# A fused transformer kernel on one core: transposes of gathered rows in another order, and three steps of VectorE moved ahead of a weight split

## The chip, the cores and the metric

The kernel runs on one core of one Trainium2 chip. The metric is the device time of one execution in microseconds (us). A core has a matmul engine (TensorE, PE in the profile; its weight loads are PEld), VectorE (DVE), ScalarE (ACT), GpSimd (POOL), SyncE (SP), which issues most DMAs, and 16 DMA engines. The engines run their own instruction streams and meet at semaphores.

## What is computed

`x` has 512 tokens of 1024 values. Three layers are added to it: attention to a context, a gated layer with ternary weights, and the one that matters here, a mixture of eight experts with a shared expert, in float32:

```python
x = x + xattn(layernorm(x), ctx)
x = x + bit_ffn(layernorm(x))
x = x + ffn(layernorm(x))

def ffn(x):                        # T = 512, D = 1024, E = 8, F = 512, K = 2
    h = rmsnorm(x)
    probs = softmax(h @ router_w)
    topv, topi = top_k(probs, 2);  topv = topv / sum(topv)
    g, u = h @ w_gate[e], h @ w_up[e]            # for each expert e
    eo = (silu(g) * u) @ w_down[e]
    moe = sum_e w_dense[:, e] * eo               # only the two chosen experts count
    sh = (silu(h @ sw_gate) * (h @ sw_up)) @ sw_down
    return moe + sh
```

## The kernel before

Each float32 matrix product is made of parts of lower precision: an operand is split into a high part (`WH`, the halves `EX[:, k, 0]` and `HTH`, copied by ACT) and a residue (`WL`, `EX[:, k, 1]`, `HTL`, made by DVE as the operand minus its high part), and PE multiplies high by high, high by low and low by high.

The expert layer works in tiles. There are four shared tiles of 128 tokens (the last of them at the end of the kernel, after the routed ones) and, with these inputs, eight routed tiles, one for each expert, of up to R = 160 gathered rows. The rows of a routed tile lie in device memory; SP loads 128 of them into `XG` and the other 32 (`TAIL_R`) into a quarter of `XY` (`XTAIL`). The order of the work is written out by hand, engine by engine, with semaphores in between.

A routed tile on PE (`routed_tile`, line 2005): the gate products into PSUM banks 0, 1, 3, 4, the up products beside them (lines 2013 to 2020), then the transposes of the *next* tile's rows (`routed_rows`, line 1940), then the down products (lines 2028 to 2044). The transposes write in three groups, `TK` = chunks 0 to 2, 3 to 5, and 6 and 7, into banks `TB` = 0, 1, 3, which the gate and up results must have left: DVE's `routed_product` (line 1027) reads them in three steps and raises `hsum` to 3 (banks 0 and 1 free), 4 (bank 3) and 5. `routed_rows` transposes 8 chunks of `XG` (line 1944, 128 rows each), then 8 chunks of the 32 rows in `XY` (line 1947), and raises `et_pe` after the first group's `XY` part and at the end. ACT copies the groups to `EX` (`routed_hi`, line 1572; the first waits for the first `et_pe`, the second for the other), DVE makes their residues (`routed_lo`, line 1014).

A routed tile on DVE (`tile`, line 1212): sums, result of the tile before, products, `routed_hidden_lo`, `routed_lo`; after it the six halves of the next expert's weight residues (`split`, line 1000). Each half is 128x2048 and raises `free_c[j]` (j = 0, 1 gate, 2, 3 up, 4, 5 down). SP's load of the following expert's half j waits for `free_c[j]`, and so do PE's products: gate for `free_c0` and `free_c1`, up for `free_c2` and `free_c3`, down for the last two.

The entry to the routed tiles is written out apart. The third shared tile is tile NS - 1 = 2. Its hidden values go to `HTKH` and `HTKL` and are kept for the end of the kernel. On PE its gate and up products are followed by the transposes of the first routed tile's rows (into banks `TB_FIRST` = 4, 5, 3) and of its own hidden values `HE` (line 1995). On DVE, lines 1202 to 1209:

```python
            split(1, 2)
            split(1, 0, (0,))
            e.wait_ge(s("rows"), 1)
            split(1, 0, (1,))
            hidden_product(NS - 1)
            routed_lo(NS, TB_FIRST)
            hidden_lo(NS - 1, HTKH, HTKL)
            split(1, 1)
```

`hidden_product` makes `HE` (line 1054), `hidden_lo` the residue `HTKL` (line 1062), `hidden` is one and then the other. ACT's `hidden` (line 1599) does the Silu, the high parts of the gate weights, the copies of `routed_hi` and then those to `HTKH` (line 1607), then splits the up weights.

Of the kernel before, what the change touches and what calls it, by code (L numbers as in the profile page):

```python
# [21 lines left out]
P = 128  # L22
# [12 lines left out]
NS = 3  # L35
R = 160
# [42 lines left out]
def program(nc, x, ctxT, wv, wqk, wo, wbit, n_gate, n_down, n_rms, wrt, wmoe, out, rows_dram):  # L79
    es = ExitStack()  # L80
    with es:
# [186 lines left out]
        def s(name):  # L268
            if name not in S:
                S[name] = sem(name)  # L270
            return S[name]
# [415 lines left out]
        def _(e):  # L687
# [515 lines left out]
            split(1, 0, (0,))  # L1203
            e.wait_ge(s("rows"), 1)
            split(1, 0, (1,))
            hidden_product(NS - 1)
            routed_lo(NS, TB_FIRST)
            hidden_lo(NS - 1, HTKH, HTKL)
            split(1, 1)
# [56 lines left out]
        def _(e):  # L1266
# [370 lines left out]
            e.wait_ge(s("ys_d"), NS)  # L1637
            e.wait_ge(s("ht_lo"), 2 * NS)
            e.wait_ge(s("cnt"), 1)
# [18 lines left out]
        def _(e):  # L1658
# [280 lines left out]

            def routed_rows(t, at=TB):  # L1940
                waits(e, ("e_in", t * 32 + 32))
                for n, ks in enumerate(TK):
                    for i, k in enumerate(ks):
                        e.transpose(bank[at[n]][:, i * R:i * R + P], XG[:, k * P:k * P + P], IDF[:, :])
                for n, ks in enumerate(TK):
                    for i, k in enumerate(ks):
                        m = e.transpose(bank[at[n]][:, i * R + P:i * R + R], XY[XTAIL, k * P:k * P + P], IDF[XTAIL, XTAIL])
                    if n != 1:
                        m.then_inc(s("et_pe"), 1)
# [11 lines left out]
            def tile(t, n, gi):  # L1961
# [18 lines left out]
                if n < NS - 1:  # L1980
                    rows_t(0, H3[:, n + 1, :])
                elif more:
                    e.wait_ge(s("ys_d"), NS)
                    routed_rows(NS, TB_FIRST)
                else:
                    waits(e, ("ys_a", t + 1), ("ys_d", t + 1), (free_c[4], gi + 1), (free_c[5], gi + 1))
                    kept_result(HT1H, HT1L, 2)
# [17 lines left out]
            def routed_tile(t, gi):  # L2005

                waits(e, ("et_lo", t * 2 + 2))
                for m in range(2):
                    waits(e, (free_c[2 * m], gi + 1), (free_c[2 * m + 1], gi + 1))
                    for f in range(KE):  # L2010
# [10 lines left out]
                        if m:  # L2021
                            mm.then_inc(s("up_pe"), 1)
                        elif f % 2:
                            mm.then_inc(s("gate_pe"), 1)
                waits(e, ("hsum", t * 5 + 4))
                routed_rows(t + 1)
                waits(e, ("ys_a", t + 1), ("ys_d", t + 1), (free_c[4], gi + 1), (free_c[5], gi + 1))
# [123 lines left out]
```

## Time and profile before

| what | us |
|---|---|
| median of 3 executions | 652.65 |
| lowest, highest | 651.95, 652.75 |
| the profiled execution: its time | 652.65 |
| its span | 650.9 |
| PE busy | 619.1 |
| DVE busy | 512.7 |
| ACT busy | 423.5 |
| POOL busy | 147.4 |

PEclk is the granted clock of TensorE as a share of 2.4 GHz (0.50 is 1.2 GHz). The time is that of the whole execution; the span runs from the first to the last recorded instruction. A busy engine is one with an instruction under way, and the ends of matmuls are modelled, so rows of PE may overlap: the start of one to the start of the next is the step to read. In a timeline row, equal instructions in a row are merged: start, time from the first start to the last end, engine, line, operation, output and inputs, active rows and columns, count. A bracket behind it tells the idle time of that engine ahead of it and what ended it; without a bracket there was none that counts.

### The profile page before, as it was taken

Reading aid. Unit: us, or ns where it says so; the run is one execution under the profiler, and the core shown is the slowest. Engines: PE = TensorE matmul, PEld = TensorE weight load, DVE = VectorE, ACT = ScalarE, POOL = GpSimd, SP = SyncE. Lnnn points to the kernel's source line nnn. Section 1 sums busy time; section 2 is a strip of 40 time slices with the busy share of each in tenths; the row PEclk is TensorE's granted clock in tenths of the full one; section 3 lists DMA queues with packets and bytes.
Section 4 is the critical chain, followed back from the end, with each engine's and each line's share of the span. In section 5 each row is a group of like instructions: output and inputs, shape, how many; then the busy total and the mean of one; then the engine's idle time right before and its main releaser. Section 6 shows DMA issues by size and latency. Waiting matters only on the chain.

```text
span 650.9 us, 10573 instructions
## 1 busy us (share of the span) xinstructions
PE 619.1 (95%) x3676; PEld 481.8 (74%) x3677; DVE 512.7 (79%) x861; ACT 423.5 (65%) x559; POOL 147.4 (23%) x146
## 2 busy tenths in 40 slices
PE   5889999998999999969999998999999999999996
PEld 4678888886887444434557888898988989889775
DVE  5787777889587779989899467678796887968686
ACT  3888888789656969885475355547375573755630
POOL 3363445426000333518900310000000000000051
PEclk9999999999999999989999998999999999999999
DMA  8967776765246999736999548595775957759247
GB/s 332 408 260 298 294 298 234 299 260 191 98 152 265 416 366 349 287 129 244 416 371 358 211 184 307 223 393 193 297 297 207 391 201 300 285 221 380 88 163 264
DMA packets 31068, 177.87 MB, mean 273 GB/s; under 512 B 4064, under 2 KB 4064, under 8 KB 14784
## 3 DMA queue, kind: packets, MB, share of 16 engines
q1 hardware_dynamic: 25536, 158.64, 63.1%
q0 software_dynamic: 5504, 18.88, 7.7%
q8 instruction: 15, 0.25, 0.2%
q14 instruction: 13, 0.11, 0.1%
HBM read 154.30 MB, written 23.20 MB: 273 GB/s over the span
## 4 chain that ended last, share of the span: by engine, by line
PE 58%; DVE 16%; ACT 13%; issue 5%; DMA 5%; POOL 1%; SPq 1%; DVEq 0%; POOLq 0%; ACTq 0%
PE BK L2017 14%; PE BK L305 9%; PE BK L2020 5%; ACT PR L1350 5%; PE BK L311 4%; PE BK L1757 4%; PE BK L312 3%; PE BK L317 3%; PE BK L1858 3%; PE BK L2040 2%; DVE WL L1004 2%; DMA RA<-wbit 2%; PE BK L2039 2%; DMA RX<-wqk 2%; DVE BH L886 1%
## 5 line engine op out<-in xcount | busy, mean ns | idle before, releaser
L2017 PE MATMUL BK<-EX,WH 128*128 128x320 f32 x512 | 133.3, 344 | 1.8 <-DVE EX L1017 1.8
L2020 PE MATMUL BK<-EX,WL 128*128 128x160 f32 x448 | 106.3, 237 | 0.0
L1004 DVE TENSOR_TENSOR WL<-RA,WH 128x2048 fp32r<-128x2048 f32 x40 | 89.3, 2286 | 9.4 <-ACT WH L1535 9.2
L2017 PEld LDWEIGHTS BK<-EX,WH 128*128 128x128 f32 x512 | 93.0, 190 | 2.7 <-issue 2.0
L2020 PEld LDWEIGHTS BK<-EX,WL 128*128 128x128 f32 x448 | 86.3, 193 | 0.3
L1535 ACT ACTIVATE WH<-RA 128x2048 fp32r<-128x2048 f32 x40 | 73.7, 1920 | 2.2 <-PE BK L1858 2.2
L681 POOL DMA_INDIRECT GA<-rows,SLOT x4 | 4.9, 1228 | 248.4 <-DVE WL L1004 247.4
L649 POOL TENSOR_TENSOR HB<-HB,ND (+2 forms) x28 | 31.1, 1128 | 104.7 <-DVE BH L886 104.0
L1420 ACT ACTIVATE RA<-RA,RT 128x2048 int16<-128x2048 f32 x22 | 44.2, 2019 | 9.4 <-DMA RA<-wbit 6.4
L1004 DVE TENSOR_TENSOR WL<-RC,WH 128x2048 fp32r<-128x2048 f32 x20 | 44.9, 2284 | 0.7 <-ACT WH L1535 0.7
L1626 ACT ACTIVATE HX<-SR 128x320 fp32r<-128x320 f32 x16 | 7.5, 471 | 54.0 <-DVE SR L1035 54.0
L1812 PE MATMUL BK<-TG,XQ 128*128 128x512 bf16 x192 | 42.4, 379 | 0.1
L1535 ACT ACTIVATE WH<-RC 128x2048 fp32r<-128x2048 f32 x20 | 37.3, 1907 | 7.5 <-PE BK L2040 6.8
L1858 PE MATMUL BK<-TD,HQT 128*128 128x512 bf16 x176 | 39.8, 387 | 0.0
L1032 DVE TENSOR_TENSOR UT<-BK,SR 128x160 f32<-128x160 f32 (+1 forms) x24 | 9.1, 380 | 35.6 <-PE BK L2017 35.6
L1350 ACT ACTIVATE PR<-BK,RT 128x512 f32<-128x512 f32 (+1 forms) x64 | 32.7, 536 | 6.6 <-DVE RT L753 6.6
L1323 ACT ACTIVATE RA<-RA 128x2048 f32<-128x2048 f32 x19 | 36.2, 1910 | 0.0
L1812 PEld LDWEIGHTS BK<-TG,XQ 128*128 128x128 bf16 x192 | 18.6, 98 | 22.5 <-ACT XQ L1413 0.6
L1812 PE MATMUL BK<-TX,XQ 128*128 128x512 bf16 x160 | 35.2, 379 | 0.0
L607 POOL TENSOR_TENSOR WQH<-RA,ONEF 128x768 fp32r<-128x768 f32 (+1 forms) x14 | 22.0, 1574 | 51.1 <-DMA RA<-wqk 43.3
L1858 PEld LDWEIGHTS BK<-TD,HQT 128*128 128x128 bf16 x176 | 17.4, 100 | 20.7 <-issue 1.4
L1812 PEld LDWEIGHTS BK<-TX,XQ 128*128 128x128 bf16 x160 | 15.7, 98 | 18.9
(305 smaller groups left out, 1582.2 us busy)
## 6 DMA issues: line engine op xcount, KB each, us to landing
RA<-wbit SPq DMA_DIRECT2D x54, 1024.0 KB, 6.4
RA<-wmoe SPq DMA_DIRECT2D x40, 1024.0 KB, 6.8
RC<-wmoe SPq DMA_DIRECT2D x20, 1024.0 KB, 7.5
rows<-ZERO POOLq DMA_DIRECT2D x40, 256.0 KB, 12.8
XG<-rows SPq DMA_DIRECT2D x10, 512.0 KB, 3.7
rows<-YS SPq DMA_DIRECT2D x9, 512.0 KB, 6.0
RA<-wqk SPq DMA_DIRECT2D x7, 640.0 KB, 7.8
RA<-wo SPq DMA_DIRECT2D x4, 1024.0 KB, 7.4
```

What stands on the lines that cost most here:

```text
L305: m = e.matmul(dst, st, mv, start=first and i == 0 and j == 0, stop=last and i == n - 1 and j == 2)
L311: e.matmul(dst, sh, mh, start=first and i == 0, stop=False)
L649: e.tensor_tensor(HB[:, t, cs], HB[:, t, cs], ND[:, cs], ALU.mult).then_inc(s("hnd"), 1)
L1004: e.tensor_tensor(WL[m][:, q * RAW:q * RAW + RAW], RC[j][:, :], WH[m][:, q * RAW:q * RAW + RAW].bitcast(f32), ALU.subtract)\
L1323: e.activation(RA[j][:, :], RA[j][:, :], ACT.Abs, accum_out=ACCW[:, column]).then_inc(free_a[j], 1)
L1350: ins = e.activation(PR[h][:, off:off + P * (i + 1)], STR[h][:, off:off + P * (i + 1)], ACT.Exp, bias=NM[:, h, i:i + 1], accum_out=RS[:, h ...
L1420: e.activation(RB16[j], RB[j][:, :], ACT.Copy, scale=SW[:, 0:1]).then_inc(s("rnd"), 1)
L1535: e.activation(WH[m][:, q * RAW:q * RAW + RAW], RC[2 * m + q][:, :], ACT.Copy)\
L1812: m = e.matmul(bank[out], XQ[:, k, t * P:t * P + P], weights[:, k, :], start=k == 0, stop=k == KD - 1)
L1858: m = e.matmul(bank[2 * (t % 2) + q], HQT[t % 2][:, k, :], (TD1[:, k, :] if k < 16 else TD2[:, k - 16, :])[:, q * 512:q * 512 + 512], star ...
L2017: mm = e.matmul(bank[GBK[f]][:, 0:2 * R], WH[m][:, at], EX[:, k, :, :].rearrange("p a b -> p (a b)"), start=k == 0, stop=k == KD - 1)
L2020: e.matmul(bank[GBK[f]][:, 0:R], WL[m][:, at], EX[:, k, 0, :], start=False, stop=False)
```

## The change

Three places are edited.

1. On PE, `routed_rows` takes the groups it is to do. Within a group each 128-row transpose of `XG` is now followed by the 32-row transpose of `XY` for the same chunk. In a routed tile the first two groups wait for `hsum` 3 and the third for `hsum` 4; before, all waited for `hsum` 4. At the entry all three groups run in one go.
2. On DVE, at the entry, `hidden_product`, `hidden_lo` and `routed_lo`, in this order, stand ahead of the second half of the gate weights' residue; before, that half came first, and `hidden_lo` last.
3. On ACT, a wait for `ht_lo` ahead of the routed tiles is gone.

```diff
--- before.py
+++ after.py
@@ -1202,10 +1202,9 @@
             split(1, 2)
             split(1, 0, (0,))
             e.wait_ge(s("rows"), 1)
+            hidden(NS - 1, HTKH, HTKL)
+            routed_lo(NS, TB_FIRST)
             split(1, 0, (1,))
-            hidden_product(NS - 1)
-            routed_lo(NS, TB_FIRST)
-            hidden_lo(NS - 1, HTKH, HTKL)
             split(1, 1)
             e.sem_inc(s("hsum"), 5 * NS)
 
@@ -1635,7 +1634,6 @@
             e.sem_inc(s("ys_a"), NS)
             split(1, NS, (1,))
             e.wait_ge(s("ys_d"), NS)
-            e.wait_ge(s("ht_lo"), 2 * NS)
             e.wait_ge(s("cnt"), 1)
             with e.Fori(1, NE) as gi:
                 n, t0 = group_of(e, gi)
@@ -1937,14 +1935,14 @@
                     m = e.transpose(bank[4 + q][:, k * P:k * P + P], rows[:, cs], IDF[:, :])
                 m.then_inc(s("et_pe"), 1)
 
-            def routed_rows(t, at=TB):
-                waits(e, ("e_in", t * 32 + 32))
-                for n, ks in enumerate(TK):
-                    for i, k in enumerate(ks):
-                        e.transpose(bank[at[n]][:, i * R:i * R + P], XG[:, k * P:k * P + P], IDF[:, :])
-                for n, ks in enumerate(TK):
-                    for i, k in enumerate(ks):
-                        m = e.transpose(bank[at[n]][:, i * R + P:i * R + R], XY[XTAIL, k * P:k * P + P], IDF[XTAIL, XTAIL])
+            def routed_rows(t, ns, at=TB):
+                for n in ns:
+                    if n == 0:
+                        waits(e, ("e_in", t * 32 + 32))
+                    for i, k in enumerate(TK[n]):
+                        cs = slice(k * P, k * P + P)
+                        e.transpose(bank[at[n]][:, i * R:i * R + P], XG[:, cs], IDF[:, :])
+                        m = e.transpose(bank[at[n]][:, i * R + P:i * R + R], XY[XTAIL, cs], IDF[XTAIL, XTAIL])
                     if n != 1:
                         m.then_inc(s("et_pe"), 1)
             def routing(step):
@@ -1981,7 +1979,7 @@
                     rows_t(0, H3[:, n + 1, :])
                 elif more:
                     e.wait_ge(s("ys_d"), NS)
-                    routed_rows(NS, TB_FIRST)
+                    routed_rows(NS, (0, 1, 2), TB_FIRST)
                 else:
                     waits(e, ("ys_a", t + 1), ("ys_d", t + 1), (free_c[4], gi + 1), (free_c[5], gi + 1))
                     kept_result(HT1H, HT1L, 2)
@@ -2022,8 +2020,10 @@
                             mm.then_inc(s("up_pe"), 1)
                         elif f % 2:
                             mm.then_inc(s("gate_pe"), 1)
+                waits(e, ("hsum", t * 5 + 3))
+                routed_rows(t + 1, (0, 1))
                 waits(e, ("hsum", t * 5 + 4))
-                routed_rows(t + 1)
+                routed_rows(t + 1, (2,))
                 waits(e, ("ys_a", t + 1), ("ys_d", t + 1), (free_c[4], gi + 1), (free_c[5], gi + 1))
                 for h in range(2):
                     waits(e, ("ht_hi", t * 2 + h + 1))
```

PE, in the loop over the routed tiles: from the last up product (L2017, L2020) over the transposes (XG: L1944, XY: L1947) to the first down product (L311). Before:

```order
843 L2017 MATMUL BK<-EX,WH_140 128x320
844 L358 REGISTER_ALU
845 L358 ISA [waits hsum]
846 L1944 MATMUL BK<-IDF,XG 128x128 [waits e_in]
847 L1944 MATMUL BK<-IDF,XG 128x128 x7
848 L1947 MATMUL BK<-IDF,XY 128x32 x8
849 L358 REGISTER_ALU [waits free_c4,free_c5,ys_d,ys_a]
850 L311 MATMUL BK<-WH_141,HX 128x512 [waits ht_hi]
```

After, the last pair of the second group, the third group and the first down product (XY is now line 1945). Ahead of these rows stand `hsum` 3, `e_in` and five pairs like the first one here:

```order
869 L1944 MATMUL BK<-IDF,XG 128x128
870 L1945 MATMUL BK<-IDF,XY 128x32
871 L358 REGISTER_ALU
872 L1944 MATMUL BK<-IDF,XG 128x128 [waits hsum]
873 L1945 MATMUL BK<-IDF,XY 128x32
874 L1944 MATMUL BK<-IDF,XG 128x128
875 L1945 MATMUL BK<-IDF,XY 128x32
876 L358 REGISTER_ALU [waits free_c4,free_c5,ys_d,ys_a]
877 L311 MATMUL BK<-WH_141,HX 128x512 [waits ht_hi]
```

Eight 128-row and eight 32-row transposes in two runs have become sixteen that alternate, with a wait before the seventh pair.

DVE, at the entry, between the weight residues of the gate (WL_146) and of the up weights (WL_150). Before:

```order
460 L1004 TENSOR_TENSOR WL_146<-RA_95,WH_145 128x2048 [waits m_hi]
461 L1004 TENSOR_TENSOR WL_146<-RA_96,WH_145 128x2048 [waits m_hi,rows]
462 L1054 TENSOR_TENSOR HE<-BK,SI 128x256 [waits up_pe,gate_a]
463 L1054 TENSOR_TENSOR HE<-BK,SI 128x256
464 L1017 TENSOR_TENSOR EX<-BK,EX 128x3x160 [waits et_hi] x2
465 L1017 TENSOR_TENSOR EX<-BK,EX 128x2x160 [waits et_hi]
466 L1062 TENSOR_TENSOR HTKL<-BK,HTKH 128x256 [waits ht_hi] x2
467 L1004 TENSOR_TENSOR WL_150<-RA_97,WH_140 128x2048 [waits m_hi]
468 L1004 TENSOR_TENSOR WL_150<-RA_98,WH_140 128x2048 [waits m_hi]
```

After:

```order
460 L1004 TENSOR_TENSOR WL_146<-RA_95,WH_145 128x2048 [waits m_hi]
461 L1054 TENSOR_TENSOR HE<-BK,SI 128x256 [waits up_pe,gate_a,rows]
462 L1054 TENSOR_TENSOR HE<-BK,SI 128x256
463 L1062 TENSOR_TENSOR HTKL<-BK,HTKH 128x256 [waits ht_hi] x2
464 L1017 TENSOR_TENSOR EX<-BK,EX 128x3x160 [waits et_hi] x2
465 L1017 TENSOR_TENSOR EX<-BK,EX 128x2x160 [waits et_hi]
466 L1004 TENSOR_TENSOR WL_146<-RA_96,WH_145 128x2048 [waits m_hi]
467 L1004 TENSOR_TENSOR WL_150<-RA_97,WH_140 128x2048 [waits m_hi]
468 L1004 TENSOR_TENSOR WL_150<-RA_98,WH_140 128x2048 [waits m_hi]
```

The second WL_146 row went from ahead of HE to behind EX, and HTKL from behind EX to ahead of it.

## Rows read from the trace of the kernel before

**Rows 1.** The page, part 1: busy time, share of the span, instructions.

```profile
PE 619.1 (95%) x3676; PEld 481.8 (74%) x3677; DVE 512.7 (79%) x861; ACT 423.5 (65%) x559; POOL 147.4 (23%) x146
```

**Rows 2.** Waits from 386 us: us in total, times, longest us.

```profile
PE BK L2017 <- DVE EX L1017: 1.8, 1, 1.8
...
PEld BK L1947 <- issue: 1.5, 9, 0.2
```

**Rows 3.** Lines from 400 us: busy us, mean ns | idle before us.

```profile
L2017 PE MATMUL BK<-EX,WH 128*128 128x320 f32 x501 | 129.0, 342 | 0.0
```

**Rows 4.** Lines 1944 and 1947: durations, first and last start.

```profile
L1944 PE MATMUL BK<-IDF,XG x72: 270/272/273, 390.7 to 605.7; 128*128 128x128 f32 x72
...
L1947 PE MATMUL BK<-IDF,XY x72: 220/222/243, 391.7 to 606.3; 32*128 32x32 f32 x72
```

**Rows 5.** Timeline, PE, first routed tile: start, us, engine, line, what.

```profile
413.56 1.04 PE L1944 MATMUL BK<-IDF,XG 128*128 128x128 f32 x8
...
414.53 0.68 PE L1947 MATMUL BK<-IDF,XY 32*128 32x32 f32 x8
...
415.14 0.50 PE L311 MATMUL BK<-WH,HX 128*128 128x512 f32 x1
```

**Rows 6.** Timeline, PE, around the 8-row transposes of the logits.

```profile
354.39 0.39 PE L311 MATMUL BK<-WH,EX 128*128 128x512 f32 x1
354.61 0.39 PE L312 MATMUL BK<-WL,EX 128*128 128x512 f32 x1
354.93 0.41 PE L1919 MATMUL BK<-IDF,HE 8*128 8x8 f32 x4
355.27 0.50 PE L311 MATMUL BK<-WH,EX 128*128 128x512 f32 x1
```

**Rows 7.** Timeline, ACT, first routed tile.

```profile
414.71 0.47 ACT L1626 ACTIVATE HX<-SR 128x320 fp32r<-128x320 f32 x1 [3.15 <-DVE SR L1035]
415.09 1.34 ACT L1576 ACTIVATE EX<-BK 128x480 fp32r<-128x480 f32 x3
```

**Rows 8.** Timeline, DVE and PE, the next expert's weight splits and its first product.

```profile
418.27 6.70 DVE L1004 TENSOR_TENSOR WL<-RA,WH 128x2048 fp32r<-128x2048 f32 x3 [0.89 <-ACT WH L1535]
...
424.43 0.31 PE L2017 MATMUL BK<-EX,WH 128*128 128x320 f32 x1
```

**Rows 9.** Timeline, PE, entry to the routed tiles.

```profile
390.72 1.03 PE L1944 MATMUL BK<-IDF,XG 128*128 128x128 f32 x8
...
392.82 0.77 PE L1995 MATMUL BK<-IDF,HE 128*128 128x128 f32 x4 [0.46 <-DVE HE L1054]
395.43 0.38 PE L2017 MATMUL BK<-EX,WH 128*128 128x320 f32 x1 [1.84 <-DVE EX L1017]
```

**Rows 10.** Timeline, DVE, entry to the routed tiles.

```profile
387.94 4.50 DVE L1004 TENSOR_TENSOR WL<-RA,WH 128x2048 fp32r<-128x2048 f32 x2 [1.57 <-ACT WH L1535]
392.35 0.75 DVE L1054 TENSOR_TENSOR HE<-BK,SI 128x256 f32<-128x256 f32 x2
393.01 1.61 DVE L1017 TENSOR_TENSOR EX<-BK,EX 128x480 fp32r<-128x480 f32 x3
394.54 0.75 DVE L1062 TENSOR_TENSOR HTKL<-BK,HTKH 128x256 fp32r<-128x256 f32 x2
```

**Rows 11.** Timeline, ACT, entry to the routed tiles.

```profile
392.08 1.36 ACT L1576 ACTIVATE EX<-BK 128x480 fp32r<-128x480 f32 x3 [2.38 <-PE BK L1947]
393.32 0.69 ACT L1607 ACTIVATE HTKH<-BK 128x256 fp32r<-128x256 f32 x2
...
401.40 0.44 ACT L1616 ACTIVATE SR<-BK 128x320 f32<-128x320 f32 x1 [2.23 <-PE BK L2017]
```

**Rows 12.** Stretch: length, PE busy (count), PEclk, DMA share, GB/s; then timeline, PE.

```profile
396.05:399.46 3.41, 3.41 (x17) 0.50 0.95 352
288.53:293.65 5.12, 4.95 (x28) 0.50 0.47 195
...
288.53 3.04 PE L1852 MATMUL BK<-IDB,HQ 128*128 128x128 bf16 x22 [5.22 <-DVE HQ L990]
```

## The prediction

> **What bounds the kernel now.** I read the page first, then the list of waits, then the timeline at the two places that the diff touches. TensorE is busy for 95% of the span [rows 1], so only what stands between its matmuls, or what it issues itself, can move the time much. In the waits from 386 us on there is one real wait of the matmul queue near the change: 1.8 us ahead of the first product of the first routed tile. The other entry, 1.5 us in nine pieces ahead of the loads of the 32-row transposes, is put down to "issue", that is, to nothing that another engine did [rows 2]. In the lines from 400 us on, the routed products have no idle time before them [rows 3]. So the eight routed tiles, one for each expert, run on TensorE without a wait. For them, semaphores set earlier buy nothing; a nanosecond more in TensorE's own stream is paid eight times.
>
> **Part 1: the order of the transposes in a routed tile.** Before, PE issues 8 transposes of XG (128 rows) and then 8 of XY (32 rows). The XG ones start at 413.56 and span 1.04 us; one lasts 0.272 us [rows 4], so seven steps take 0.77 us, 0.11 us each, and the last starts at 414.33. The XY ones start at 414.53 and span 0.68 us with 0.222 us each: 0.066 us a step, the last at 414.99. The next product starts at 415.14 [rows 5]. From first transpose to next product: 1.58 us. Now look at the two seams. From the last XG to the first XY there are 0.20 us where a step is 0.11, from the last XY to the next product 0.15 us where a step is 0.066. Each change of the number of active rows costs about 0.09 us. That this belongs to the row count, and not to this place, shows elsewhere. The 8-row transposes of HE start 0.32 us after the last 128x512 product, where such products follow each other at 0.23 us: again 0.09. On the way back, (0.41 - 0.20)/3 = 0.07 us a step puts the last one at 355.14, and the next product comes at 355.27: 0.13 where a step is 0.07, so 0.06 [rows 6].
>
> The change makes the order XG, XY, XG, XY and so on: 15 seams inside the block and one behind it, where there were 1 and 1. That is 14 more. At 0.09 us: +1.26 us for a tile, and the block takes 2.84 us instead of 1.58. It lies on the path, because TensorE is what everything else waits for. Eight tiles: **+10.1 us**. Bounds: nothing, if the seams hide when they alternate (rival A); the 0.06 of the 8-row case for the seven additional ways back, 7 x 0.03 x 8 = 1.7 us less. Above: the second XY after a seam may itself be slow, but in the new order there is no second one; I let the upper bound be 1 us more. I take 0.09 because both seams of these very instructions show it.
>
> The Trainium skill, page "TensorEngine Tiling (Array Packing)", section "Tiling Modes", Key Properties, says that changing the tiling mode, "not just tile", drains TensorE. By that rule every seam of a 128-row and a 32-row instruction costs, as the rows have it; the page gives no price, and the 0.09 us is the trace's.
>
> **Part 2: the earlier wait in a routed tile.** The first six transpose pairs wait for `hsum` 3 instead of 4, the last two pairs for 4. The old wait never held PE: the transposes at 413.56 have no idle time before them [rows 5]. The gain is 0. The added wait stands in the middle of PE's stream, with the down products queued behind it. Its cost lies between 0 and the 0.17 us of an issue gap [rows 2], 0 to 1.4 us over eight tiles; the similar wait in the middle of the up products (line 2012, with L2017 right behind it) leaves L2017 no idle time at all from 400 us on [rows 3], so I take **+0.2 us** in all.
>
> Who profits from the first `et_pe` coming earlier? ACT can copy the first group only after its own HX copy, which waits for DVE until 414.71 and lasts to 415.18; the EX copies follow at once at 415.09 [rows 7]. So an increment before 415.09 is worth nothing. The second `et_pe` comes when all pairs are done, 1.26 us later than now; ACT's second and third copy, and DVE's, end about 1.0 us later. What they hold up next is the split of the next expert's gate weights: DVE runs three halves in 6.70 us from 418.27, so the second ends near 422.8, and PE needs it at 424.43 [rows 8]: 1.6 us of slack. DVE moves by 1.0 us, PE by 1.26: the slack stays. Cost 0. It would be lost only if DVE came 1.9 us later.
>
> **Part 3: the entry to the routed tiles.** Before: PE ends the shared tile, does the 16 routed transposes from 390.72, waits 0.46 us for HE, transposes HE at 392.82 and stands idle for 1.84 us until 395.43 [rows 9]. DVE runs two weight halves 387.94 to 392.44, then HE 0.75 us, the EX residues 1.61 us, the HTK residues 0.75 us [rows 10]. ACT copies EX 392.08 to 393.44 and HTKH 393.32 to 394.01 [rows 11].
>
> Now the second weight half (gate weights, `free_c1`) stands behind all of that, and PE's first routed product waits for `free_c0`, `free_c1` and `et_lo`. Working forward:
> - DVE ends the first half near 390.2. HE needs the shared tile's up product, which ends when the transposes begin to run, near 390.9, so HE is done at 391.7, 1.4 us earlier.
> - PE: pairs at 0.35 us from 390.72. The third pair's XY starts at 391.63 and ends at 391.85 (first `et_pe`); the eighth's starts at 390.72 + 7 x 0.35 + 0.20 = 393.4 and ends at 393.6 (second `et_pe`). The HE transposes follow at 393.54 and are through at 393.9 and 394.15.
> - ACT: first EX copy 391.9 to 392.4; the other two from 393.65 to 394.5; HTKH to 394.8 and 395.15.
> - DVE waits for HTKH, since its residues are now first in the queue: HTKL 394.9 to 395.6, EX residues to 397.15, the weight half (4.50 / 2 = 2.25 us) to 399.4.
> - PE starts at 399.5 instead of 395.43: **+4.05 us**.
>
> Queued behind on DVE are the two halves of the up weights, which then end near 404; PE needs them after all gate products, of which the first half alone took from 395.43 to 401.40 [rows 9, 11], so not before 405.5: nothing. On SP the load of the next expert's second weight half waits for `free_c1` and moves by 7 us, with four loads behind it; they are issued by about 404, and DVE's splits use them only from 418.27 on [rows 8]. Nothing. The wait that ACT loses (`ht_lo`) held nothing: ACT's next work followed its own split without idle time.
>
> **The clock.** After the 1.84 us gap the granted clock was 0.50 from 396.05 to 399.46: 3.4 us, half of it lost, 1.7 us. After the 5.22 us gap ahead of 288.53 it was 0.50 until 293.65: 5.1 us of work, 2.5 us lost [rows 12]. The new gap is 394.15 to 399.5, 5.3 us, nearest to the second. The difference is +0.8 us; the step down need not fall at the same point of the work, so -0.9 to +1.0; I take **+0.5 us**.
>
> **Sum.** The profiled execution took 652.65 us, its span is 650.9, and 652.65 is also the median, so no correction is needed. 652.65 + 10.1 + 0.2 + 4.05 + 0.5 = **667.5 us**. The end of the kernel (the copies of the last tile's result, its store, the gathers) waits for PE's last routed tile and shifts with it.
>
> **Rivals.**
> A. *The seams hide.* Alternating loads could be brought in under the running transpose, and a pair would cost no more than 0.11 + 0.066. For it: at both places the trace has one seam each way, never a row of them. Against: the loss shows at every seam. Then the tiles cost nothing and the entry is shorter (transposes done at 392.4, HTKH at 393.9, the EX residues at 395.9, the weight half at 398.1): +2.8 + 0.5, 656.0 us. The Trainium skill, "TensorE: Matmul & The Clock Gate", "Step-by-step: what each phase is for", says that weight loads are pulled ahead of running matmuls when row groups do not conflict or the load goes to the background buffer; taken alone, that gives this case. 7%.
> B. *The clock falls in the routed tiles too.* The block would have 2.84 us of short instructions with gaps. The clock did fall after thin work at the entry. Against: there PE had idle time of 0.46 and 1.84 us, here gaps of 0.09. One fall of 3.4 us a tile costs 1.7 us, eight cost 13.7: 681 us; a few of them, 670 to 675. 9%.
> C. *Faster.* If alternating lets each XY transpose run under the load of the next XG one, a pair costs little more than the 0.11 of its XG part, say 0.13: a block takes about 1.1 us, -0.5 us a tile, -4.0 in all, against +2.8 at the entry with no change of the clock: 651.4 us. It wins from 0.35 us a tile on, that is, a pair under 0.155 us. Against it: the seams cost, they don't save. 2%, and 1% for a time within the bound of no change.
> D. *The entry does not move as worked out*, for instance because PE's own scalar loads ahead of the loop, and not DVE, held it until 395.43. That would not help: DVE's half ends at 399.4 either way. It is inside the range.
>
> **How the numbers follow.** The forecast, 81%: 667.5 us. Within it: seams -1.7 to +1, the added wait -0.2 to +1.2, the clock -1.4 to +0.5, the entry +-0.5. Not all fall on one side, so 663.8 to 671; A and C lie below, most of B above. What a measurement of this kernel can tell from no change is about 0.2%, 1.3 us. Slower 0.97 (forecast, A, B), same 0.01, faster 0.02.
>
> **What would show it.** In the trace after: between the first XG transpose of a routed tile and the first down product 2.8 us instead of 1.58, starts of XG and XY alternating at 0.20 and 0.15 us; the distance of two routed tiles 28.6 instead of 27.3 us (now: the last XG transpose of all starts at 605.7 [rows 4], its block 0.77 us earlier, seven tiles behind 413.56); the first routed product about 4 us later, released by the DVE weight split and not by EX; DVE idle ahead of HTKL for some 3 us; the granted clock 1 in all routed tiles but the first. Wrong: pairs at 0.18 us, or DVE's weight splits being what PE waits for at later tiles.

## The result

| | us |
|---|---|
| before, median of 4 | 652.7 (651.95 to 653.28) |
| after, median of 4 | 684.38 (683.93 to 686.18) |
| ratio | 1.0491, 95% interval 1.0469 to 1.0514 |
| after, the profiled execution: its time, its span | 685.42, 683.6 |

The change makes the kernel 31.7 us slower. The forecast was 667.5 us and the range ended at 671: the direction and the two places were right, the size was half of what came. The cause that I had as rival B, at 9%, came true in every tile, and the price of a seam (the place in TensorE's stream where 128-row and 32-row instructions meet) was too low.

The page of the profile after, PE's busy time and the granted clock in 40 slices. Against [rows 1] PE is busy 30 us longer, as 95% of a longer span. The 7 in the second half of the clock's row is the entry to the routed tiles. The falls in the tiles can't be seen in this row: one of 3.4 us takes a tenth from a slice of 17.1 us, and 9 stands for 90% or more. They show only in shorter stretches, further down.

```profile
PE 649.1 (95%) x3663; PEld 498.8 (73%) x3677; DVE 513.6 (75%) x861; ACT 424.6 (62%) x559; POOL 148.3 (22%) x146
...
PEclk9999999999999999899999979999999999999999
```

The waits from 386 us on (engine, line, waited for: us in total, times, longest). PE's one wait at the entry has grown from the 1.8 us of [rows 2] to 5.3, and its releaser is now the weight split. ACT now waits for PE's transposes in every tile, 15.4 us in all with the entry. In the tiles that costs nothing, since no routed product behind the entry waits for it, but it shows how late the second `et_pe` is.

```profile
ACT EX L1575 <- PE BK L1945: 15.4, 10, 2.4
...
PE BK L2015 <- DVE WL L1004: 5.3, 1, 5.3
```

PE in the first routed tile: start, us, line. Where [rows 5] had eight and eight, each instruction now stands alone.

```profile
419.63 0.27 PE L1944 MATMUL BK<-IDF,XG 128*128 128x128 f32 x1
419.83 0.24 PE L1945 MATMUL BK<-IDF,XY 32*128 32x32 f32 x1
420.01 0.33 PE L1944 MATMUL BK<-IDF,XG 128*128 128x128 f32 x1
420.27 0.24 PE L1945 MATMUL BK<-IDF,XY 32*128 32x32 f32 x1
...
422.87 0.24 PE L1945 MATMUL BK<-IDF,XY 32*128 32x32 f32 x1
423.05 0.50 PE L311 MATMUL BK<-WH,HX 128*128 128x512 f32 x1
```

From 419.63 to 423.05 are 3.42 us where there were 1.58. The first XG to XY is 0.20 us, as I had reckoned; XY to XG is 0.18 instead of 0.15, and every later XG to XY is 0.26 instead of 0.20. A pair costs 0.435 us, not 0.35. The XG transposes themselves are recorded longer, 0.328 us in the median against 0.272 [rows 4]: each but the first of a block now comes right behind a change of the row count.

```profile
L1944 PE MATMUL BK<-IDF,XG x72: 270/328/331, 390.7 to 637.7; 128*128 128x128 f32 x72
```

The last of these starts at 637.7; its block began 3.04 us (seven pairs) earlier, at 634.7, so seven tiles take (634.7 - 419.6) / 7 = 30.7 us each, where they took 27.3. Of the 3.4 us more, 1.84 are the block. The other 1.55 are the clock. Stretches of PE (length, busy and count, granted clock, DMA share, GB/s):

```profile
400.05:406.60 6.55, 6.55 (x27) 0.50 0.90 331
406.60:423.60 17.00, 17.00 (x120) 1.00 0.61 241
423.60:427.00 3.40, 3.40 (x10) 0.51 0.57 192
427.10:454.40 27.30, 27.30 (x178) 1.00 0.68 254
454.40:457.80 3.40, 3.40 (x10) 0.50 0.63 193
```

After the entry the clock is 0.50 for 6.55 us of work, against 3.4 us in [rows 12]. Then it falls behind the first block, from 423.6 to 427.0, is 1 again, falls from 454.4 to 457.8, and so on: eight falls behind eight blocks, the last at 638.7. Each begins 4.0 us after the first transpose of its block, behind the first full products, and holds 3.4 us of work at half the clock. In the trace before there was none between 399.5 and the end of the tiles.

The entry, against [rows 10], [rows 11] and [rows 9]: DVE, ACT, PE.

```profile
391.00 0.76 DVE L1054 TENSOR_TENSOR HE<-BK,SI 128x256 f32<-128x256 f32 x2 [0.79 <-PE BK L317]
395.43 0.76 DVE L1062 TENSOR_TENSOR HTKL<-BK,HTKH 128x256 fp32r<-128x256 f32 x2 [3.67 <-ACT HTKH L1606]
396.10 1.61 DVE L1017 TENSOR_TENSOR EX<-BK,EX 128x480 fp32r<-128x480 f32 x3
397.62 4.49 DVE L1004 TENSOR_TENSOR WL<-RA,WH 128x2048 fp32r<-128x2048 f32 x2
```

```profile
394.22 0.90 ACT L1575 ACTIVATE EX<-BK 128x480 fp32r<-128x480 f32 x2 [1.60 <-PE BK L1945]
395.00 0.67 ACT L1606 ACTIVATE HTKH<-BK 128x256 fp32r<-128x256 f32 x2
```

```profile
390.70 0.27 PE L1944 MATMUL BK<-IDF,XG 128*128 128x128 f32 x1
...
393.94 0.24 PE L1945 MATMUL BK<-IDF,XY 32*128 32x32 f32 x1
394.11 0.65 PE L1993 MATMUL BK<-IDF,HE 128*128 128x128 f32 x4
400.05 0.60 PE L2015 MATMUL BK<-EX,WH 128*128 128x320 f32 x1 [5.29 <-DVE WL L1004]
```

DVE idles 3.67 us between HE and HTKL, waiting for ACT's HTKH, which stands behind EX copies that wait for the second `et_pe`; the second half of the gate weights ends at 397.62 + 2.25 = 399.87, and PE starts at 400.05. The HE transposes come at once (394.11, no idle time), as forecast; the first product is 4.6 us later than at 395.43.

### The profile page after: what moved, and what is told of

Its sections match the earlier page's. It is cut to its first block, busy times and chain, and to the rows that moved or that the text cites. A ratio compares the mean times of both kernels' runs of the same rounds, so it can differ in the third digit from the quotient of the medians.

```text
span 683.6 us, 10567 instructions
## 1 busy us (share of the span) xinstructions
PE 649.1 (95%) x3663; PEld 498.8 (73%) x3677; DVE 513.6 (75%) x861; ACT 424.6 (62%) x559; POOL 148.3 (22%) x146
## 4 chain that ended last, share of the span: by engine, by line
PE 61%; DVE 15%; ACT 12%; DMA 4%; issue 4%; POOL 1%; SPq 1%; DVEq 0%; POOLq 0%; ACTq 0%
PE BK L2015 14%; PE BK L305 9%; PE BK L2018 5%; PE BK L311 5%; ACT PR L1349 5%; PE BK L312 4%; PE BK L317 3%; PE BK L1755 3%; PE BK L1856 3%; PE BK L1944 3%; PE BK L2040 2%; PE BK L1945 2%; DVE WL L1004 2%; PE BK L2039 2%; DMA RA<-wbit 2%
## 5 line engine op out<-in xcount | busy, mean ns | idle before, releaser
L2015 PE MATMUL BK<-EX,WH 128*128 128x320 f32 x512 | 134.7, 347 | 5.3 <-DVE WL L1004 5.3
L1004 DVE TENSOR_TENSOR WL<-RA,WH 128x2048 fp32r<-128x2048 f32 x40 | 89.3, 2287 | 10.3 <-ACT WH L1534 10.1
L649 POOL TENSOR_TENSOR HB<-HB,ND (+2 forms) x28 | 31.1, 1126 | 104.6 <-DVE BH L886 103.9
L1349 ACT ACTIVATE PR<-BK,RT 128x512 f32<-128x512 f32 (+1 forms) x64 | 32.7, 536 | 6.6 <-DVE RT L753 6.6
L311 PE MATMUL BK<-WH,HX 128*128 128x512 f32 x64 | 33.4, 523 | 0.0
```

What stands on the lines that cost most here:

```text
L311: e.matmul(dst, sh, mh, start=first and i == 0, stop=False)
L649: e.tensor_tensor(HB[:, t, cs], HB[:, t, cs], ND[:, cs], ALU.mult).then_inc(s("hnd"), 1)
L1004: e.tensor_tensor(WL[m][:, q * RAW:q * RAW + RAW], RC[j][:, :], WH[m][:, q * RAW:q * RAW + RAW].bitcast(f32), ALU.subtract)\
L1349: ins = e.activation(PR[h][:, off:off + P * (i + 1)], STR[h][:, off:off + P * (i + 1)], ACT.Exp, bias=NM[:, h, i:i + 1], accum_out=RS[:, h ...
L2015: mm = e.matmul(bank[GBK[f]][:, 0:2 * R], WH[m][:, at], EX[:, k, :, :].rearrange("p a b -> p (a b)"), start=k == 0, stop=k == KD - 1)
```

## Experiments

Each ratio is against executions of the kernel before on the same chip, with its 95% interval.

### The two parts alone

`e1_dve_order` is the kernel before with the second edit alone:

```diff
-            split(1, 0, (1,))
-            hidden_product(NS - 1)
-            routed_lo(NS, TB_FIRST)
-            hidden_lo(NS - 1, HTKH, HTKL)
+            hidden(NS - 1, HTKH, HTKL)
+            routed_lo(NS, TB_FIRST)
+            split(1, 0, (1,))
```

> The kernel before with the change of VectorE's order at the entry alone; TensorE's stream is that of before. Theory (the entry and the tiles add up, and the clock falls in the tiles because the alternating transposes are thin work): VectorE's HTKL residues wait for ScalarE until about 394, the gate weights' second half ends near 398.3, and the first routed product starts 2.9 us later than before; with a longer low clock after it about +0.8: 656.4 us, and the granted clock is 1 in all later tiles. Rival (the entry's new order shifts the routed tiles against the clock and so makes it fall in each of them): the clock falls about once a tile here too, at 1.5 us each, near 668 us.

Measured: 656.55 us, ratio 1.006 (1.0043 to 1.0078), +4.0 us. Its DVE at the entry, and PE over the routed tiles:

```profile
391.36 0.76 DVE L1054 TENSOR_TENSOR HE<-BK,SI 128x256 f32<-128x256 f32 x2 [0.79 <-PE BK L317]
394.10 0.76 DVE L1062 TENSOR_TENSOR HTKL<-BK,HTKH 128x256 fp32r<-128x256 f32 x2 [1.99 <-ACT HTKH L1606]
394.77 1.61 DVE L1017 TENSOR_TENSOR EX<-BK,EX 128x480 fp32r<-128x480 f32 x3
396.30 6.69 DVE L1004 TENSOR_TENSOR WL<-RA,WH 128x2048 fp32r<-128x2048 f32 x3
...
404.00:619.00 215.00, 215.00 (x1447) 1.00 0.72 272
```

The weight half ends near 396.30 + 2.2 = 398.5 and PE starts at 398.72. Counted from the first XG transpose (391.06 here, 390.72 before) the first product comes after 7.66 instead of 4.71 us: +2.95, and the low clock lasts for 1 us more of work. The clock is 1.00 in all tiles: the entry does not make it fall later. The rival is out. The first block starts 3.8 us later than before (417.32 against 413.56), which agrees with the measured +4.0.

`e6_alt_onewait` is the first edit alone, without its new wait: all sixteen transposes alternate behind `hsum` 4. Abridged, with the increments of `et_pe` left out:

```diff
-                for n, ks in enumerate(TK):
-                    for i, k in enumerate(ks):
-                        e.transpose(... XG chunk k ...)
-                for n, ks in enumerate(TK):
-                    for i, k in enumerate(ks):
-                        m = e.transpose(... XY chunk k ...)
+                for n, ks in enumerate(TK):
+                    for i, k in enumerate(ks):
+                        e.transpose(... XG chunk k ...)
+                        m = e.transpose(... XY chunk k ...)
```

> The kernel before with the XG and XY transposes alternating, one wait (hsum 4) ahead of all, and VectorE's order as before. Theory: the block is 3.41 us instead of 1.58 in each of eight tiles and the clock falls in each at about 1.5 us, together 26.7; the entry starts about 1.2 us later, since the second et_pe comes later, and holds the low clock longer by about 1: 681.6 us. Rival (the entry's order makes the clock fall): only the blocks, 8 x 1.84 = 14.7, and the entry: about 669 us with the clock at 1 in the tiles. Rival (the additional wait in the middle of the stream is what hurts): no loss here, about 653 us.

Measured: 679.58 us, ratio 1.0407 (1.0383 to 1.043), +27.1 us. The clock over the tiles is that of eight falls:

```profile
403.00:640.00 237.00, 237.00 (x1421) 0.94 0.68 248
```

27.1 and 4.0 add up to 31.1, against 31.7 for both together. The block takes 3.41 us here as in the changed kernel, so the new wait in the middle of PE's stream costs nothing measurable. The wait dropped on ACT was never run alone; with the other leftovers it lies in the 0.6 us between 31.1 and 31.7.

### What a seam costs

`e3_groups3` and `e4_runs2` have one wait and DVE's order of before, and cut the two runs of eight into shorter ones; `e11_runs112` begins with four pairs and ends with two runs of two and two. Abridged:

```diff
+                for size in (3, 3, 2):        # e4: (2, 2, 2, 2); e11: (1, 1, 1, 1, 2, 2)
+                    (XG transposes of the next `size` chunks, then their XY transposes)
```

> The kernel before with the transposes in runs: three XG, three XY, three XG, three XY, two XG, two XY; one wait. Six changes of the row count in a block instead of two. Theory (a change of the row count costs 0.09 to 0.15 us, whatever the order): +0.4 to +0.55 us a block, 3 to 4.5 us in all, and the block of about 2.0 us is not thin enough for the clock to fall: 656 to 657.5 us. Rival (any thinning makes the clock fall): about 12 us more, 668.

> The kernel before with runs of two XG and two XY transposes, eight changes of the row count in a block. From 1.57 us with two changes, 2.10 with six and 3.41 with sixteen I expect 2.36 to 2.4 us a block (0.13 for each change more): +6.5 us in eight tiles and about 0.8 at the entry, 660 us with the clock at 1 in the tiles. If a block of this kind is already thin enough for the clock to fall: about 12 more, 672.

> VectorE's order as before, four alternating pairs and then two runs of two and two: 12 changes of the row count, a block of 2.9 us. Theory: +1.3 us in each of eight tiles and about 1 at the entry: 664 us without falls of the clock. If the clock falls in a tile depends on how much of the thin stretch lies together and on where the step falls in it, some of the tiles will show it, between none and eight at 1.5 us each: 664 to 676 us, and where a fall comes once it comes in the tiles after it too, as in the run with the narrow transposes four times over.

`e3_groups3` was expected at 656 to 657.5 us, `e4_runs2` at 660, `e11_runs112` at 664 without falls; all three came within 1.3 us. PE in the first routed tile of `e3_groups3`:

```profile
412.71 0.49 PE L1945 MATMUL BK<-IDF,XG 128*128 128x128 f32 x3
413.13 0.37 PE L1948 MATMUL BK<-IDF,XY 32*128 32x32 f32 x3
413.43 0.55 PE L1945 MATMUL BK<-IDF,XG 128*128 128x128 f32 x3
413.91 0.37 PE L1948 MATMUL BK<-IDF,XY 32*128 32x32 f32 x3
```

The second XG run lasts 0.55 us where the first lasts 0.49. This is the part of a seam that shows only behind it: the first instruction after a change is itself recorded longer, here by 0.06 us, and the next one starts that much later.

| kernel | changes of the row count within the block and behind it | block, us | time, us | granted clock over the tiles, profiled execution |
|---|---|---|---|---|
| before | 2 | 1.57 | 652.5 | 1.00 |
| e3_groups3 | 6 | 2.10 | 656.43 | 1.00 |
| e4_runs2 | 8 | 2.37 | 658.75 | 1.00 |
| e11_runs112 | 12 | 2.88 | 664.98 | 1.00 |
| e6_alt_onewait | 16 | 3.41 | 679.58 | 0.94 |

The block grows by (3.41 - 1.57) / 14 = 0.131 us for each change, in a straight line that begins with runs of three: the price does not depend on the order being an alternation. The times of the first four follow from it: 8 x 0.53 = 4.2 against +3.9 measured, 8 x 0.80 = 6.4 against +6.2, 8 x 1.31 = 10.5 against +12.0, of which some belong to the entry (the executions of `e11_runs112` spread from 662.34 to 665.95, and the profiled one is the fastest of them; the mean granted clock of the others is 0.987 to 0.989 against its 0.991, so a fall or two more, somewhere, are possible). The last one stands off the line by about 12 us: those are the falls of the clock.

What a seam is, the weight loads show. In the trace before, the loads of the XG transposes lie ahead of their matmuls (the first at 413.44 for 413.56), but the first load of the XY transposes starts as late as its own matmul, 414.52 for 414.53 [rows 5]. The idle time of the load queue that [rows 2] put down to "issue", nine times up to 0.2 us, is this seam:

```profile
414.52 0.57 PEld L1947 LDWEIGHTS BK<-IDF,XY 32*128 32x128 f32 x8 [0.17 <-issue]
```

In the changed kernel it is so at every instruction of the block but the first:

```profile
420.01 0.14 PEld L1944 LDWEIGHTS BK<-IDF,XG 128*128 128x128 f32 x1
```

Its matmul starts at 420.01 too. A change of the active columns has no such price: in the down products of the trace before, 128 active columns (420.53), 64 (420.75), 32 (420.98) and 32 again (421.22) follow each other at 0.22 to 0.24 us, and products of 128 columns throughout at 0.23 us.

### Row count or alternation

`e5_alt_full` alternates, but never changes the row count: each XY step uses all 128 rows of XY and picks the 32 with 32 columns of the identity, as an ordinary float32 product. `e7_full` does the same steps in two runs of eight. GpSimd clears XY once before it is used.

```diff
-                        m = e.transpose(out, XY[XTAIL, chunk], IDF[XTAIL, XTAIL])
+                        m = e.matmul(out, XY[:, chunk], IDF[:, XTAIL], start=True, stop=True)
```

> XG and XY alternate as in the changed kernel, one wait, VectorE's order as before, but each XY step takes all 128 rows of XY as the stationary operand and 32 columns of the identity as the moving one, as an ordinary product, so that the number of active rows never changes (GpSimd clears XY once ahead of the gathers being read). Theory (the row count is what costs): no seams, a block of about 1.5 us or less, no fall of the clock in the tiles, 651.5 to 654 us. Rival (alternating itself, or two sources of the stationary operand in turn, is what costs): near 681 us like the alternation with 32 rows.

> As e5_alt_full (XY steps as ordinary products over 128 rows), but all eight XG transposes first and then the eight XY steps, so nothing alternates. Theory (alternating as such is free, only a change of the row count costs): the block is as long as in e5_alt_full, 2.25 us, and the time is the same within 1 us, 657 to 658.5 us. Rival (alternating costs something of its own): the block is shorter than 2.0 us and the time 654 to 655.5 us.

Measured: 657.8 us (1.0086, 1.0067 to 1.0105) and 659.01 us (1.0093, 1.0067 to 1.0119). Both miss their numbers, for a reason that the rows show. PE in `e5_alt_full`:

```profile
412.93 0.30 PE L1946 MATMUL BK<-IDF,XG 128*128 128x128 f32 x1
413.07 0.31 PE L1949 MATMUL BK<-IDF,XY 128*128 128x32 f32 x2
413.21 0.31 PE L1946 MATMUL BK<-IDF,XG 128*128 128x128 f32 x1
```

Each XY step has become two matmuls (x2), which the transpose was not, and a block has 24 matmuls instead of 16. It takes 2.25 us alternating and 2.58 us in two runs, so the time over before is about that of the blocks: 8 x 0.68 = 5.4 and 8 x 1.01 = 8.1 against +5.3 and +6.4 measured. (The 1.7 us by which `e7_full` is shorter fit one fall of the clock fewer: three of its four executions have a mean granted clock of 0.994, those of before on the same chip 0.987 to 0.991.) The question itself is answered. With the row count constant, an alternating pair of XG and XY takes 0.28 us with its three matmuls, against 0.435 us with two matmuls and the change of rows, and alternating is 0.33 us a block cheaper than two runs, not dearer. The changes of the row count cost; alternation does not. The clock stays at 1 in the tiles of both.

### What makes the clock fall

`e8_wide3` and `e9_narrow4` keep the two changes of before and lengthen a run: the eight XG transposes three times over, or the eight XY transposes four times over. Abridged:

```diff
+                for rep in range(3):          # e8: around the XG transposes
                    (eight XG transposes)
+                for rep in range(4):          # e9: around the XY transposes instead
                    (eight XY transposes)
```

> The order of before (XG, then XY, two changes of the row count), but the eight XG transposes are issued three times over, so that the block is about 3.3 us long without gaps. What makes the clock fall: if a long stretch of transposes counts as thin work, whatever the gaps, the clock falls in the tiles: 1.74 x 8 + 1.5 + 12 = 680 us. If it is the idle time at the changes of the row count, it stays at 1: 668 us.

> The order of before, but the eight XY transposes (32 rows, 32 columns) are issued four times over: two changes of the row count, 0.063 us a step, a block of about 3.1 us whose steps stream few columns. If few columns in a stretch are enough to make the clock fall: 1.5 x 8 + 1.3 + 12 = 678 us. If only idle time at the changes does it: 666 us.

Measured: 668.6 us (1.0252, 1.022 to 1.0283) and 670.87 us (1.0289, 1.0256 to 1.0323). PE in a tile and over the tiles of `e8_wide3`, then of `e9_narrow4`:

```profile
411.57 2.78 PE L1945 MATMUL BK<-IDF,XG 128*128 128x128 f32 x24
...
414.89 0.50 PE L311 MATMUL BK<-WH,HX 128*128 128x512 f32 x1
...
400.00:626.00 226.00, 226.00 (x1557) 1.00 0.70 264
```

```profile
414.38 1.04 PE L1945 MATMUL BK<-IDF,XG 128*128 128x128 f32 x8
415.35 1.68 PE L1955 MATMUL BK<-IDF,XY 32*128 32x32 f32 x24
416.87 0.66 PE L1948 MATMUL BK<-IDF,XY 32*128 32x32 f32 x8
...
400.40:533.40 133.00, 133.00 (x985) 1.00 0.71 275
533.50:536.90 3.40, 3.40 (x10) 0.50 0.64 193
...
598.40:649.00 50.60, 49.97 (x298) 1.00 0.50 183
```

In the profiled execution of `e8_wide3` a block of 3.32 us, nearly all of it 128-column transposes, leaves the clock at 1 in all tiles. The other three executions were 2.7 to 5.2 us slower, at a mean granted clock of 0.986 to 0.988 against its 0.995. By an estimate from these numbers that is some three falls of 3.4 us more; before and behind the tiles they can lie too (the profiled one lacks even the fall at the entry), and where they lie is not recorded. So wide transposes do not make the clock fall in every tile, but that they never do is not shown.

In `e9_narrow4` a shorter block, 3.07 us, with 32-column transposes and no more seams than before, leaves the clock at 1 behind the first four blocks. It falls behind the fifth, sixth and seventh, at 533.5, 564.2 and 594.9, where the distance to the next block is 30.4 instead of 28.8 us, and not behind the eighth, which starts at 621.0. So more idle time at seams is not needed; my second expectation for `e9_narrow4` (idle time only) is refuted, and the first one (falls everywhere) came behind three blocks of eight. The eight blocks are the same instructions with the same 3.07 us. What else decides whether the clock falls, perhaps where in time a block lies, the runs don't show.

`e10_apart` keeps all sixteen changes of `e6_alt_onewait`, but three pairs stand ahead of the last quarter of the up products. Abridged:

```diff
                         if m and f % 2 == 0:
                             waits(e, ("hsum", t * 5 + f // 2 + 1))
+                        if m and f == KE - 1:
+                            waits(e, ("hsum", t * 5 + 3))
+                            (three alternating pairs, first group)
...
-                (eight alternating pairs)
+                (five alternating pairs)
```

> The alternation of e6_alt_onewait (16 changes of the row count in each tile, VectorE's order as before), but the first three pairs stand ahead of the last quarter of the up products, with a wait for hsum 3, and the other five behind it: the thin stretch of 3.4 us is cut into 1.3 and 2.1 us with 2 us of full products in between. Theory (the changes cost 1.84 us a tile in any case, and the clock falls because they lie together): the clock stays at 1 in the tiles; 652.7 + 14.7 + 2.2 at the entry, whose transposes still lie together, = 669.6 us. Rival (any 16 changes in a tile make the clock fall): 681 us.

Measured: 668.68 us, ratio 1.0244 (1.0228 to 1.0259). The two blocks take 1.25 and 2.11 us, 3.36 together, nearly the 3.41 of `e6_alt_onewait`; yet the clock over the tiles is 1:

```profile
401.00:632.00 231.00, 231.00 (x1451) 1.00 0.67 259
```

The same transposes in the same order, with the same number of changes, are 10.9 us faster than in `e6_alt_onewait` (11.4 us, if each is counted from the kernel before on its own chip: +15.7 and +27.1). What differs is that 2.2 us of full products stand between the two blocks. All four executions of `e10_apart` have a mean granted clock of 0.988 to 0.992, all four of `e6_alt_onewait` 0.971 to 0.974. That is the clock's share, separated from the seams'.

### A version faster than both

At the entry PE stood idle for 1.84 us, put down to DVE's EX residues [rows 9]. But these end at 393.01 + 1.61 = 394.62, and PE started at 395.43. What filled the time was PE's own sequence: between the last HE transpose and the first product it loads the two counts of the first expert's tiles. In the trace before, these loads of PE's sequencer (16, two for each expert; min, median and longest in ns) begin at 393.4, and the first pair holds the longest:

```profile
L352 PEldq TENSOR_LOAD <-CNT x16: 296/305/490, 393.4 to 585.5; - x16
```

`e13_hoist` loads them ahead of the wait for HE, and the first expert's tile stands outside the loop over the experts; `e14_hoist_fill` adds ten transposes behind HE's that compute nothing.

```diff
+                if n == NS - 1:
+                    e.wait_ge(s("cnt"), 1)
+                    first_group.append(group_of(e, 1))
                 for h in range(2):
                     e.wait_ge(s("eh"), t * 2 + h + 1)
...
+            for k in range(10):               # e14 only
+                e.transpose(bank[1][:, 0:P], HE[:, k % KE * P:k % KE * P + P], IDF[:, :])
+            n, t0 = first_group[0]
+            with e.Fori(0, n) as i:
+                routed_tile(t0 + i, 1)
-            with e.Fori(1, NE) as gi:
+            with e.Fori(2, NE) as gi:
```

> A try to beat the kernel before, from what the entry showed: TensorE's two scalar loads of the tile counts stand, for the first expert, ahead of its wait for HE instead of behind it, where 2 us passed between the last HE transpose and the first routed product. Theory: the first product is then held by VectorE's EX residues alone and starts at about 394.8 instead of 395.4, 0.6 us earlier; the low clock after the gap may stay: 652.1 us against 652.7. Rival: TensorE's loads then delay the HE transposes instead: no change or 1 us slower.

> As e13_hoist, and ten more 128-row transposes of HE into a bank that nobody reads stand in the gap behind the HE transposes (1.1 us of work that computes nothing). Theory (the clock falls at the entry because of the thin stretch around the gap): the granted clock does not fall behind it or falls more rarely, which gives back up to 1.7 us: 650.4 to 652 us. Rival (filling does nothing for the clock): as e13_hoist, 652.1 us.

Measured: 651.13 us, ratio 0.9973 (0.9958 to 0.9987), and 649.75 us, ratio 0.9955 (0.9941 to 0.9968). PE at the entry of `e13_hoist` with its clock behind it, and PE at the entry of `e14_hoist_fill`:

```profile
390.92 1.03 PE L1944 MATMUL BK<-IDF,XG 128*128 128x128 f32 x8
...
393.02 0.77 PE L1998 MATMUL BK<-IDF,HE 128*128 128x128 f32 x4 [0.46 <-DVE HE L1054]
394.88 0.41 PE L2020 MATMUL BK<-EX,WH 128*128 128x320 f32 x1 [1.09 <-DVE EX L1017]
...
395.20:399.90 4.70, 4.70 (x39) 1.00 0.94 312
```

```profile
393.26 0.77 PE L1998 MATMUL BK<-IDF,HE 128*128 128x128 f32 x4 [0.47 <-DVE HE L1054]
393.87 1.25 PE L2091 MATMUL BK<-IDF,HE 128*128 128x128 f32 x10
395.12 0.42 PE L2020 MATMUL BK<-EX,WH 128*128 128x320 f32 x1
```

From the first XG transpose to the first product `e13_hoist` takes 3.96 us instead of 4.71: 0.75 us won (0.6 was expected), and the idle time has gone from 1.84 to 1.09. The EX residues, which end near 394.8 in this trace, now release the product at 394.88 in fact. The edit moves the wait for `cnt` and the start of the loop together with the loads, so what each of them is worth is not separated. In its profiled execution the clock did not fall behind the entry either: the first block starts 20.5 us after the first XG transpose, where it was 22.8. `e14_hoist_fill` has no idle time left there and the same 3.97 us. Its median is 1.4 us lower still, but the two intervals overlap, and the profiled executions of both are without the fall: whether the filling does more than the earlier start is open.

## Why the prediction was wrong, and where it was right

- **The step that failed first: the price of a seam.** I counted only the gap ahead of the first instruction behind a change, 0.09 us. That instruction is recorded longer too and holds up the next one, whatever its row count, so each change costs 0.13, and a block +1.84 us instead of +1.26. The trace before held this, and I passed it over: the first XY transpose behind the change lasts 243 ns, the median 222 [rows 4], and the first product behind the way back 0.50 us where its like last 0.39 [rows 6]. I wrote that the second one may be slow, but in the new order "there is no second one". There is no second one of the same kind, but the next instruction pays in its place. Eight tiles: 14.7 us instead of 10.1, 4.6 us short.
- **The step that failed most: the clock in the tiles,** which the sum put at nothing. Rival B had the mechanism, the length of a fall (3.4 us) and nearly the time (681 us; measured 684.4), but 9%. I argued that gaps of 0.09 us are not like idle times of 0.46 and 1.84 us. The runs show eight falls behind eight blocks; `e9_narrow4` shows that the clock can fall without more seams, `e10_apart` that the same work apart is harmless. That B's 681 us comes so near is partly luck: it has the seams at 10.1 us, 4.6 too low, and a fall at 1.7, a little too high. A tile is 30.7 - 27.3 = 3.4 us longer, of which 1.84 are the block and 1.55 the fall; eight falls are 12.4 us.
- **The entry: right.** Forecast +4.05, measured +4.6; the difference is the dearer seams again, which delay the second `et_pe` (ACT's second EX copy starts at 394.22 instead of the 393.65 that I had). The order of events, DVE's idle time ahead of HTKL (3.67 us for "some 3") and the new releaser are those of the working. Case D was partly true, PE's own sequence did hold it until 395.43, and, as said there, without effect on this change; it was worth 0.75 us by itself in `e13_hoist`.
- **The clock at the entry: too small.** Forecast +0.5 us. The low clock holds 6.55 us of work instead of 3.4, and the first block starts 6.1 us later (419.63 against 413.56), 1.5 more than the 4.6 of the entry.
- **The added wait: nothing**, where I had 0.2; the "issue gap" of 0.17 us that bounded it was the seam itself. The earlier `hsum`, the earlier first `et_pe` and the wait dropped on ACT gave nothing that shows, as forecast; the slack of the weight splits held: no later gate product waits for them.
- **Rival A** (seams hide) is refuted by the straight line of `e3_groups3` to `e6_alt_onewait`, **rival C** (faster) with it. The weight loads say why: behind a change the load is not brought in under the running transpose, it starts with its own matmul. The Trainium skill, "TensorEngine Tiling (Array Packing)", section "Tiling Modes", Key Properties, says that changing the tiling mode drains TensorE. The runs agree where the row count changes: 0.13 us a change, and no loss from alternating with the row count held in `e5_alt_full`. The drain itself is not seen in a trace; seen is that the weight load comes late.

The sum with the measured terms: 14.7 (blocks) + 12.4 (falls in eight tiles) + 4.6 (entry) + 1.5 (clock at the entry) = 33.2, against 32.7 us between the spans. What makes the clock fall behind these blocks, in terms that would forecast it for another block, stays open: in the profiled executions it fell behind all of 3.41 us with 16 changes, behind three of eight of 3.07 us with 32-column transposes, and behind none of 2.88 us or less, nor of 3.32 us with 128-column ones.

## What to carry to other kernels

Keep matmuls of equal row count together: an order that looks neater in the source can cost 0.13 us at every seam on the engine that bounds the kernel. Price such a change up to the second instruction behind it, not the first. And where a change lengthens a stretch of small work on TensorE, look at the stretch as a whole: the same instructions cost 11 us less with full products between them.

## What was unexpected of the hardware

- The granted clock fell without more idle time than before: 32 transposes of 32 columns in a row, 3.07 us with the 128-column ones ahead of them, were enough behind three blocks of eight; 24 transposes of 128 columns and 8 of 32, 3.32 us, did not do it in the profiled execution.
- An ordinary float32 product with 32 moving columns ran as two matmuls, each with its own weight load (144 for 72), where the transpose of the same data ran as one.
- TensorE's own scalar loads, with the start of its loop, delayed the first product by 0.75 us, in a row that puts the whole wait down to VectorE.
- A change from 128 to 32 active rows or back cost 0.13 us, a change of the active columns between 128, 64 and 32 nothing that shows.
